# Ones in the last normalised column: biases carried by the weights instead of added by products and seeds

## What is computed

```python
# x: (4, 2048, 256), fp32; 8 experts of 256 x 256, top 2; 16 heads of 16
def ffn(x, We, be, Wg, bg):
    gates = softmax(x @ Wg + bg)
    top, idx = top_k(gates, 2); top = top / sum(top)
    out = einsum('nd,edo->neo', x, We) + be
    return sum(out[idx] * top)
def attn(x, Wp, bp, Wq, bq, Wk, bk, Wv, bv, Wo, bo):
    xp = x @ Wp.T + bp
    q, k, v = (xp @ Wq.T + bq) / 4, xp @ Wk.T + bk, xp @ Wv.T + bv
    # each position attends to itself and its two neighbours (cyclic)
    return softmax(q . k[i-1, i, i+1]) v[i-1, i, i+1] @ Wo.T + bo
x = x + 0.5 * ffn(layernorm(x))
x = x + attn(layernorm(x))
x = x + 0.5 * ffn(layernorm(x))
```

## Time and profile before

| | |
|---|---|
| time of three runs | 1078.8, 1081.26, 1081.43 us; median 1081.26 |
| profiled execution | 1078.79 us, its span 1076.9 us |
| mean granted TensorE clock | 0.994 of full |
| HBM read / written | 12.46 / 8.39 MB |

### The profile page before, as it was taken

The page is one execution under the profiler, slowest core; times in us unless marked ns, Lnnn a source line. Parts: engine busy times, 40 slices in busy tenths (PEclk is TensorE's granted clock), DMA queues, the critical chain, the costliest instruction groups (busy, mean ns, idle before and its releaser), DMA issues.

```text
span 1076.9 us, 17752 instructions
## 1 busy us (share of the span) xinstructions
PE 1027.7 (95%) x5277; PEld 846.0 (79%) x5277; DVE 863.5 (80%) x2405; ACT 544.0 (51%) x1219; POOL 713.4 (66%) x956
## 2 busy tenths in 40 slices
PE   4899999999999999999999999999999999999785
PEld 3687788888888888888888888888888888887563
DVE  3659888988878898888888888888888888888882
ACT  4365555555445555554455555445555554544331
POOL 3375577766667776766777776677777666664453
PEclk9999999999999999999999999999999999999998
DMA  5011000000000000000000000000000000000000
GB/s 171 11 33 36 13 20 20 21 15 7 20 20 21 20 22 11 10 21 20 20 20 21 20 1 21 20 20 21 21 21 1 21 20 20 11 10 11 10 11 20
DMA packets 12615, 23.04 MB, mean 21 GB/s; under 512 B 2244, under 2 KB 5844, under 8 KB 12520
## 3 DMA queue, kind: packets, MB, share of 16 engines
q1 hardware_dynamic: 9240, 13.37, 3.5%
q0 software_dynamic: 3280, 8.53, 2.8%
HBM read 12.46 MB, written 8.39 MB: 19 GB/s over the span
## 4 chain that ended last, share of the span: by engine, by line
PE 86%; DVE 8%; issue 2%; DMA 1%; ACT 1%; SPq 0%; POOL 0%; POOLq 0%; ACTq 0%; DVEq 0%
PE ffn_bank L1007 20%; PE ffn_bank L1009 20%; PE ffn_bank L1008 20%; PE tr_bank L1040 5%; PE mix_bank L1007 4%; PE mix_bank L1009 4%; PE mix_bank L1008 4%; PE tr_bank L1053 3%; PE mix_bank L1085 1%; DMA we_raw<-in_L_ffn_We 1%; PE tr_bank L1007 1%; PE tr_bank L1008 1%; PE tr_bank L1009 1%; DVE chain_sum L737 1%; DVE score L769 1%
## 5 line engine op out<-in xcount | busy, mean ns | idle before, releaser
L1007 PE MATMUL ffn_bank<-we_hi,T_hi 128*128 128x512 f32 x1024 | 409.5, 400 | 4.2 <-DVE chain_sum L737 3.8
L1009 PE MATMUL ffn_bank<-we_hi,T_lo 128*128 128x512 f32 x1024 | 401.0, 392 | 0.0
L1008 PE MATMUL ffn_bank<-we_lo,T_hi 128*128 128x512 f32 x1024 | 400.0, 391 | 0.0
L488 ACT ACTIVATE we_raw<-ffn_bank,gate 128x256 f32<-128x256 f32 x512 | 207.3, 474 | 163.6 <-PE ffn_bank L1009 119.9
L346 POOL TENSOR_TENSOR chain_sum<-chain_sum,we_raw 128x512 f32<-128x512 f32 x128 | 166.2, 1299 | 117.6 <-DVE chain_sum L737 115.0
L1007 PEld LDWEIGHTS ffn_bank<-we_hi,T_hi 128*128 128x128 f32 x1024 | 192.5, 188 | 44.3 <-DVE chain_sum L737 5.5
L1009 PEld LDWEIGHTS ffn_bank<-we_hi,T_lo 128*128 128x128 f32 x1024 | 192.2, 188 | 41.8
L1008 PEld LDWEIGHTS ffn_bank<-we_lo,T_hi 128*128 128x128 f32 x1024 | 192.7, 188 | 35.0
L737 DVE SCALAR_TENSOR_TENSOR chain_sum<-ffn_bank,gate,we_raw 128x256 f32<-128x256 f32 x256 | 111.6, 476 | 54.8 <-ACT we_raw L488 35.1
L737 DVE SCALAR_TENSOR_TENSOR chain_sum<-ffn_bank,gate,chain_sum 128x256 f32<-128x256 f32 x256 | 111.4, 476 | 36.9 <-PE ffn_bank L1009 36.8
L323 POOL TENSOR_TENSOR var_eps<-mean_var,eps 128x2 f32<-128x2 f32 x96 | 28.3, 295 | 152.2 <-DVE mean_var L658 152.2
(11 more groups left out here) (128 smaller groups left out, 1652.1 us busy)
## 6 DMA issues: line engine op xcount, KB each, us to landing
out_x<-y SPq DMA_DIRECT2D x31, 256.0 KB
we_raw<-in_L_ffn_We SPq DMA_DIRECT2D x2, 1024.0 KB, 13.8
x_in<-in_L_attn_x,x_row POOLq DMA_INDIRECT x60
x_in<-in_L_attn_x SPq DMA_DIRECT2D x2, 256.0 KB, 7.6
moved_qk<-qk SPq DMA_DIRECT2D x4, 124.0 KB
...
```

The lines of the kernel that those rows point to most:

```text
L488: last = nc.scalar.activation(scaled[:, f, t, half, j], ffn_bank[b][:, j * D:(j + 1) * D], ACT.Copy, scale=gate[:, 2 * f + t, e:e + 1])
L1007: nc.tensor.matmul(dest, hi[:, t, k, :], w_hi_[:, k, c0:c1], start=(first and k == 0), stop=False, skip_group_check=not first)
L1008: nc.tensor.matmul(dest, hi[:, t, k, :], w_lo_[:, k, c0:c1], start=False, stop=False, skip_group_check=not first)
L1009: last = nc.tensor.matmul(dest, lo[:, t, k, :], w_hi_[:, k, c0:c1], start=False, stop=(k == KB - 1), skip_group_check=not first)
```

## The change

Column 255 of the three normalised tensors is set to one once by GpSimd (`normed[:, ln, :, LAST:D]`), and ScalarE normalises 255 columns. In the weights the last row is replaced by the bias, and the old last row is taken off all others: for `We` by VectorE with `we_last`, its last row loaded into all partitions; for `Wg` with `wg_last`; for Wp by its last column, with bp in its place, and the bias of q, k and v is added in row 255 of the product by one more matrix product of a single row (`last_row`, `bqkv_row`). The bias products, the transpose of the gates, `gate_parts`, `base`, `bias_sum`, the seeds and the biases' preparation go. `sum_step` adds the layer's input itself, so `x_in` has four slots instead of two. Waits are on semaphores of their own at the start. The list of TensorE's steps keeps its order otherwise, but that the fourth bank of the next pair's first half is computed at the end of a filling round and not at the start of the next. The loads of `We` are one broadcast of 128x8x256, one half of 128x8x256, one of 127x8x256 and the row of `be`.

```diff
-GATE_OPS = 14
+GATE_OPS = 12
+LAST = D - 1
...
-            for k in range(KB):
-                sp.dma_start(we_raw[:, k, :].rearrange("p (e n) -> p e n", e=E),
-                             We[:, k * PART:(k + 1) * PART, :].rearrange("e p n -> p e n")).then_inc(we_loaded[k], 16)
+            sp.dma_start(we_last[:].rearrange("p (e n) -> p e n", e=E), We[:, LAST, :].partition_broadcast(PART)).then_inc(last_loaded, 16)
+            sp.dma_start(we_raw[:, 0, :].rearrange("p (e n) -> p e n", e=E),
+                         We[:, 0:PART, :].rearrange("e p n -> p e n")).then_inc(we_loaded[0], 16)
+            sp.dma_start(we_raw[0:PART - 1, 1, :].rearrange("p (e n) -> p e n", e=E),
+                         We[:, PART:LAST, :].rearrange("e p n -> p e n")).then_inc(we_loaded[1], 16)
+            sp.dma_start(we_raw[PART - 1:PART, 1, :], be.rearrange("(o e) n -> o (e n)", o=1)).then_inc(we_loaded[1], 16)
...
-                eng.wait_ge(x_gathered[n.slot], 32 * (n.const // 2))
+                eng.wait_ge(x_gathered[n.const % 4], 32 * ((n.const - 2) // 4 + 1))
...
+            for ln in (LN1, LN2, LN3):
+                nc.gpsimd.memset(normed[:, ln, :, LAST:D], 1.0)
...
-                pool.dma_start(bp_col[:, k:k + 1], bp.rearrange("(k p) -> p k", p=PART)[:, k:k + 1]).then_inc(bp_loaded, 16)
+                pool.dma_start(wp[:, k, LAST:D], bp.rearrange("(k p) -> p k", p=PART)[:, k:k + 1]).then_inc(bp_loaded, 16)
             for w, b_ in enumerate((bq, bk, bv)):
-                pool.dma_start(bqkv[:, w * D:(w + 1) * D], b_.partition_broadcast(PART)).then_inc(bqkv_loaded, 16)
-            pool.dma_start(wg_raw[:], Wg.rearrange("(k p) e -> p k e", p=PART)).then_inc(small_loaded, 16)
-            pool.dma_start(be_raw[:], be.partition_broadcast(PART // E)).then_inc(small_loaded, 16)
-            pool.dma_start(bo_all[:], bo.partition_broadcast(PART)).then_inc(small_loaded, 16)
+                pool.dma_start(bqkv_row[:, w * D:(w + 1) * D], b_.rearrange("(o n) -> o n", o=1)).then_inc(bqkv_loaded, 16)
+            pool.dma_start(wg_raw[:, 0, :], Wg[0:PART, :]).then_inc(wg_loaded, 16)
+            pool.dma_start(wg_raw[0:PART - 1, 1, :], Wg[PART:LAST, :]).then_inc(wg_loaded, 16)
+            pool.dma_start(wg_raw[PART - 1:PART, 1, :], bg.rearrange("(o e) -> o e", o=1)).then_inc(wg_loaded, 16)
+            pool.dma_start(wg_last[:], Wg[LAST, :].partition_broadcast(PART)).then_inc(wg_loaded, 16)
+            pool.dma_start(bo_all[:], bo.partition_broadcast(PART)).then_inc(bo_loaded, 16)
             pool.wait_ge(consts_set, 1)
-            for f in range(NF):
-                pool.dma_start(bg_col[2 * E * f:2 * E * f + E, 0:1], bg.rearrange("(e o) -> e o", o=1)).then_inc(small_loaded, 16)
...
-            def base_step(f, n):
-
-                if f == FFN1:
-                    await_x(pool, n)
-                else:
-                    pool.wait_ge(x2_done, n.times(1, 1))
-                pool.wait_ge(bias_copied[f], n.times(1, 1))
-                await_(pool, sum_done[f], n.times(2 * RESIDUAL_SUMS))
-                nc.gpsimd.tensor_tensor(base[:, f], (x_in if f == FFN1 else x2)[:, n.slot], bias_sum[:, f],
-                                        ALU.add).then_inc(base_done[f], 1)
-
...
-                pool.wait_ge(base_done[f], n.times(1, 1))
-                nc.gpsimd.tensor_tensor(pool_sum[:, f, t], chain_sum[:, f, t, 0], base[:, f, t], ALU.add).then_inc(done, 1)
+                if f == FFN1:
+                    await_x(pool, n)
+                    residual = x_in[:, n.const % 4, t]
+                else:
+                    pool.wait_ge(x2_done, n.times(1, 1))
+                    residual = x2[:, n.slot, t]
+                nc.gpsimd.tensor_tensor(pool_sum[:, f, t], chain_sum[:, f, t, 0], residual, ALU.add).then_inc(done, 1)
...
-            def gateT_step(g):
-                act.wait_ge(gateT_done, g.times(1, 1))
-
-                await_(act, bias_done[FFN1], min(g.const, PAIRS) if g.reg is None else g.times(1))
-                await_(act, bias_done[FFN2], (g - 5).times(1))
-                nc.scalar.copy(gateT[:], gateT_bank[:, 0:PART]).then_inc(gateT_copied, 1)
...
-                    nc.scalar.activation(normed[:, ln, t], source[:, n.slot, t], ACT.Identity,
+                    nc.scalar.activation(normed[:, ln, t, 0:LAST], source[:, t, 0:LAST], ACT.Identity,
                                          scale=rstd[:, ln, t:t + 1], bias=shift[:, ln, t:t + 1]).then_inc(normed_done[ln], 1)
-
-            def bias_step(f, n):
-                act.wait_ge(bias_done[f], n.times(1, 1))
-                await_(act, base_done[f], n.times(1))
-                nc.scalar.copy(bias_sum[:, f].rearrange("p t n -> p (t n)"), bias_bank[f][:, :]).then_inc(bias_copied[f], 1)
...
-            def seed_step(n):
-
-                if n.const == 0:
-                    act.wait_ge(bias_set, 1)
-                    act.wait_ge(setup_dve, 7)
-                readers = [(bias_copied[FFN1], n.const + 2) if (n + 1).within(PAIRS) else (v_copied, n.const),
-                           (bias_copied[FFN2], n.const - 3) if (n - 4).within(GROUPS) else (qk_copied, 2 * n.const)]
-                for t, (read, value) in enumerate(readers):
-                    await_(act, read, value)
-                    nc.scalar.copy(mix_bank[t][:, :], bqkv[:, 0:2 * D]).then_inc(qk_seeded, 1)
...
-                    after(12)
-                    await_(dve, gateT_done, g.times(1))
-                    nc.vector.tensor_copy(gate_parts[:, cs, 0:4:2, :].bitcast(f32r),
-                                          gate[:, cs].unsqueeze(2).to_broadcast([PART, nf, 2, E])).then_inc(ops, 1)
-                    after(13)
-                    nc.vector.tensor_tensor(gate_parts[:, cs, 1:4:2, :], gate[:, cs].unsqueeze(2).to_broadcast([PART, nf, 2, E]),
-                                            gate_parts[:, cs, 0:4:2, :], ALU.subtract).then_inc(ops, 1)
...
+            dve.wait_ge(wp_loaded, 16)
+            for mb in range(KB):
+                last = nc.vector.tensor_scalar(out=wp[:, mb, 0:LAST], in0=w_raw[:, 4, mb, 0:LAST],
+                                               scalar1=w_raw[:, 4, mb, LAST:D], scalar2=None, op0=ALU.subtract)
+            last.then_inc(wp_set, 1)
...
+            dve.wait_ge(last_loaded, 16)
+            dve.wait_ge(we_loaded[0], 16)
+            nc.vector.tensor_tensor(we_raw[:, 0, :], we_raw[:, 0, :], we_last[:], ALU.subtract).then_inc(we_set, 1)
+            dve.wait_ge(we_loaded[1], 16 * 2)
+            nc.vector.tensor_tensor(we_raw[0:PART - 1, 1, :], we_raw[0:PART - 1, 1, :], we_last[0:PART - 1, :],
+                                    ALU.subtract).then_inc(we_set, 1)
+                dve.wait_ge(we_hi_done, k + 1)
+                nc.vector.tensor_tensor(we_lo[:, k, :], we_raw[:, k, :], we_hi[:, k, :].bitcast(f32), ALU.subtract).then_inc(we_lo_done, 1)
...
+                    if db == KB - 1:
+                        last = nc.tensor.matmul(bank[:, 0:c1 - c0], last_row[:], bqkv_row[:, c0:c1], start=False, stop=True)
...
-            def gateT_step(s):
-                pe.wait_ge(gate_ops, (s + 1).times(GATE_OPS, GATE_OPS))
-                if s.const > 3:
-                    pe.wait_ge(lo_done[TO], after_group(s - 3))
-                await_(pe, lo_done[TB], after_pair(s - 1))
-                nc.tensor.transpose(gateT_bank[:, 0:PART], gate_parts[:].rearrange("p c k e -> p (c k e)"),
-                                    ident[:]).then_inc(gateT_done, 1)
-
-            def bias_step(f, s):
-
-                if s.reg is None and s.const == -1:
-                    pe.wait_ge(setup_dve, 7)
-                    pe.wait_ge(masks_set, 2 * NF * 2)
-                pe.wait_ge(gateT_copied, (s + 1).times(1, 1))
-                if f == FFN1:
-                    await_(pe, v_copied, (s - 1).times(1, 1))
-                else:
-                    await_(pe, qk_copied, after_pair(s - 1, 2))
-                if s.reg is None:
-                    await_(pe, bias_copied[f], (s + 1 if f == FFN1 else s - 4).times(1))
-                for t in range(2):
-                    last = nc.tensor.matmul(bias_bank[f][:, t * D:(t + 1) * D], gateT[:], be_rows[:, 2 * f + t, :],
-                                            start=(t == 0), stop=True, skip_group_check=(t == 1))
-                last.then_inc(bias_done[f], 1)
-
             def ffn_step(f, n, s, t, banks=range(4)):
                 i = T_OF_FFN[f]
+                if f == FFN1 and n.const == 0:
+                    pe.wait_ge(we_lo_done, KB)
+                    pe.wait_ge(wqkv_lo_done, KB)
                 pe.wait_ge(lo_done[i], n.times(1, 1))
                 for b in banks:
...
-                pe.wait_ge(qk_seeded, n.times(2, t + 1))
-                product(mix_bank[t][:, :], TB, n, t, wqkv_hi, wqkv_lo, 0, 2 * D, first=False).then_inc(qk_done, 1)
+                if t == 0:
+                    await_(pe, v_copied, n.times(1))
+                else:
```

(6 more changed lines are left out.)

211 lines of the change are left out of this document (71 added, 140 removed).

## The result

Before 1081.09 us (median; 1078.8 to 1081.43), after 1088.05 us (1087.73 to 1089.87, 4 runs): ratio 1.0068, 95% interval 1.0053 to 1.0084. The change makes the kernel 7 us slower. Forecast was 15 slower, 1096 in a range of 1087 to 1106: the sign, the place and the mechanism of the loss came as said and the time lies at the lower edge of the range, but the difference was forecast twice too large.

A forecast was written before the change was run, and what follows sets the result against it. TensorE's queue was taken to bound the middle, and a one-engine load to delay the start: 37.3 + 1.9 - 23.8 = +15.4 us, on the median 1081.3 giving 1096.7, stated as 1096, range 1087 to 1106.

The forecast's parts named there:

- the forecast's 23.8: Whole kernel outside the start: 23.8 us saved, 15.6 in the steady steps and 8.2 in fill and drain.
- first rival: Start: the 127-partition transfer is spread over many DMA engines after all, giving 1059.7 us, faster; chance 0.12.
- The start, 37.3 + 1.9 - 1.2: First FFN product 37.3 us later, half-rate clock costs 1.9, first round's removed wait, transpose and bias products save 1.2.
- the forecast 8.5: Start, behind the load: three VectorE passes of 2.2 us and `wqkv_lo` of 1.9 before the first FFN product.
- The clock and the removed wait: First round: FFN products beginning at 1.2 GHz lose 1.9 us; removed wait, transpose and bias products save 1.2.
- The forecast "20.2": Start: TensorE's product of Wp and wT, with the bias row's products adding 1.3, ends at 20.2 us.
- The steady part, 15.6: 26 steady steps: TensorE loses one transpose and four bias products, 0.60 us a step, 15.6 us saved.
- The drain, steps 31 to 34, forecast 0.4 + 1.5: Step 31 saves 0.4 us on TensorE; steps 32 to 34 save 0.5 each without GpSimd's `base` beside VectorE's products.
- The other small terms: Savings of 1.4 us at step 0, 0.7 in steps 1 and 2, 1.0 in steps 3 and 4, 2.0 in the last step.
- The base of the sum: Whole time: +15.4 us on the profiled 1078.8 gives 1094.2, on the median 1081.3 gives 1096.7; 1096 was forecast.

The follow-up runs named there:

- 112+15: The changed kernel with only its 127-partition load of `We` cut into 112 and 15 partitions: 1053.99 us, ratio 0.9761 to the kernel before.

## Why the prediction was right or wrong

**What it had right.** That TensorE's queue sets the middle; that the change gains 23 us outside the start (22.6 of the forecast's 23.8; 26.2 by the table); that one load of 127 partitions goes to one DMA engine and costs more than that; that 24 GB/s is its rate, from rows of 31 partitions (22 with the same load in the kernel before); that everything in the first round stands behind it. With 112+15, which is the prediction's first rival made real, the time is 1054, where the rival's sum said 1059.7.

**The start, 37.3 + 1.9 - 1.2, measured 35.75.** The half was usable at 59.35, not 61.5. The stretches show 0.07 already from 17 us on: the transfer was alone on its engine sooner than 18, and took about 42 us, near the 43 forecast. The chain behind it took 8.65 us (59.35 to 68.00) for the forecast 8.5. The clock and the removed wait together were 0.5 (10.27 from the first FFN product to the mark, against 9.74) for the forecast 0.7 (1.9 less 1.2). The forecast "20.2" for the end of the Wp product was wrong, 22.84: the bias row's two groups of products took 1.05 and 0.62 us by their starts, not 1.3 in all, and the product itself ran slowly. Here the transfer hid this, which was luck; with 112+15 it is on the path.

**The steady part, 15.6, measured 14.7**: 0.567 us a step for 0.60.

**The drain, steps 31 to 34, forecast 0.4 + 1.5, measured 4.9.** This is the term that was mis-sized, and by step it is the 1.5 of steps 32 to 34. From mark to mark the four steps took 25.98, 25.45, 21.04 and 19.43 us before, and 25.58, 23.23, 19.90 and 18.29 after: 0.4 for step 31, as forecast, and 4.5 for the other three. The prediction named the cause, GpSimd's `base` beside VectorE's products, put it between 0 and 1.3 a step and took 0.5. The trace of before held the answer: products of 3.0 to 3.2 us beside it, which after the change take 1.9 to 2.1. That is 1.1 in each of three steps, 31 to 33, and what VectorE loses in 31 shows in 32. The two kernels with the addition put back, early (0.3) and beside the products (2.4), show this. The remaining 1.2 us stay open; TensorE's bias products and ScalarE's copies are gone from these steps too, and no run parts them.

**The other small terms** (step 0, steps 1 to 4, the last step) came out 1.4 us better together.

**The base of the sum.** The terms came to +15.4, the spans say +9.6, the medians +7. The last difference is mostly the profiled execution before: at 1078.8 it was 2.3 below its median, while that after, 1088.34, is within 0.3 of its own. The sum belonged to 1078.8, and putting it on the median added 2.3. So of the 8 us that the forecast was too high, 3.0 are the drain, 2.3 the start, 2.3 the choice of base and 1.4 the small terms, less 0.9 for the steady part. Nearly all of them err to one side.
